# Query and key blocks transposed by VectorE and DMAs instead of TensorE, in a fused attention and feed-forward kernel

## The chip, the cores and the metric

The kernel runs on one core of one Trainium2 chip. The metric is the device time of one execution in microseconds. Three runs of the kernel before took 2517.53, 2520.3 and 2519.74 us; the median is 2519.74. One more execution was profiled; it took 2519.57 us, of which the profile covers a span of 2517.8.

## The reference

The input x has 4096 tokens (4 x 1024) of 512 features, all in fp32. Three residual stages follow one another:

```python
x = x + 0.5 * ffn(layernorm(x), W1, W2, W3)
x = x + attention(layernorm(x), wq, wk, wv, wo, inv_freq)
x = x + 0.5 * ffn(layernorm(x), W1, W2, W3)      # the same weights again

# ffn: hidden = silu(x @ W1.T) * (x @ W3.T)      # 2048 wide
#      return fwht(hidden) @ W2.T                # Walsh-Hadamard transform along the 2048
# attention: q, k, v of 16 heads of 32, rotary embedding on q and k;
#      scores = einsum('bshd,bstd->bsht', q, k) / sqrt(32)
#      return (softmax(scores) @ v) @ wo.T
```

The scores run over the heads of one token (s is kept, h meets t), so attention is a 16 x 16 product for each token, and no token meets another.

## The kernel before

**Tiling.** The tokens are cut into 8 tiles of 512, each of four blocks of 128 tokens; block g is block g % 4 of tile g // 4, 32 blocks in all. There are 16 passes (`PASSES`, 0 to 15), one for each tile and feed-forward stage, and the attention of the tiles is spread between them. Every matmul operand is kept as two fp32r parts, a high one (a copy that rounds) and a low one (the difference), and a product is three matmuls (`products`, L583 to L585: high x high, high x low, low x high).

**One pass.** `feed_forward(p)` has 16 steps, one for each 128 of the 2048 hidden features. In step n TensorE makes the up projections of the step, 24 matmuls of 128x512 into two banks of `gu`, then the down projection of the step before, 12 matmuls into the four banks of `acc`. ScalarE does SiLU from `gu` into `gated` (L1031), VectorE multiplies by the other bank (L1525, semaphore `s_h`), ScalarE copies the product as the high part of `hid` (L1039), VectorE subtracts for the low part (L1532, `s_hid_lo`), and TensorE uses both in the down projection. At the end of a pass the up projections of step 15 come first, then the down projections of steps 14 and 15 one after the other; only the last one (L583 to L585 into `acc`) waits at its start for the low part of step 15. SyncE loads each step's weights from device memory into two slots, about one step ahead.

**Attention on VectorE.** TensorE has only the projections. Scores and mixing of a block are 16 units on VectorE, each one product (L1258 or L1263) and one sum (L1270 or L1272) of 128x1024. `UNITS` says which units a pass has, and `units_by_step` deals them out over steps 0 to 14 so that VectorE's load is even, with costs for what stands beside them (`beside`): 2.5 for a unit, 0.55 for normalising a block at step 13. The exp of a block is on ScalarE, after the table load that it needs, and SiLU loads its own table again after it.

**The blocks of queries and keys.** For the pass p `new_subs(p)` lists two or three blocks whose queries, keys and values are projected in the gap before it. The first two are early (`early_subs`) when their first feed-forward stage is long done, 23 blocks in all. An early block is normalised by VectorE at step 13 of the pass ahead, into `prod[:, 2]` (`ln_apply`, L1174). TensorE transposes it in four squares of 128 (`transpose_sub`, L664) into PSUM, ScalarE copies that as the high part of `sub_xt` (`sub_high`, L915), VectorE subtracts for the low part (`sub_low`, L1138), and the projections of queries, keys and values use them. Where the transposes stand in TensorE's order depends on the gap: before a pass in `LATE` (3, 5, 7, 14) they are in `late_gap`, between the second and the third block of the output projection; else they are at the end of the pass ahead, between the up projections of step 15 and the down projection of step 14. One block is early before passes 2, 9 and 11, two before 3, 4, 5, 6, 7, 8, 10, 12, 13 and 14.

**The input of the feed-forward** goes another way already, where its pass isn't late (`MOVED`, nine passes): VectorE normalises it at steps 8 and 9, transposes it in squares of 32 (L1504), ScalarE issues four DMAs in each of steps 10 to 13 (`move`, L925), which put the squares in place within SBUF, ScalarE copies the high part at step 14 (`moved_high`, L932), and VectorE subtracts at step 15 (L1510).

Each engine runs its instructions in the order of the program. ScalarE issues DMAs from the same queue as its activations.

## Time and profile before

| | |
|---|---|
| median of three runs | 2519.74 us |
| the profiled execution, its span | 2519.57 us, 2517.8 us |
| TensorE matmuls busy | 2504.8 us (99%) |
| TensorE weight loads busy | 2074.0 us (82%) |
| VectorE busy | 2027.5 us (81%) |
| ScalarE busy | 528.8 us (21%) |
| GpSimd busy | 63.6 us (3%) |
| DMA queue of SyncE, of ScalarE: share of 16 engines | 45.8%, 3.4% |

A row of the profile names the line, the engine, the operation and what it writes and reads (out<-in). PE is TensorE, DVE VectorE, ACT ScalarE, POOL GpSimd, SP SyncE; ACTq and SPq are the DMA issues on those engines' queues. Matmuls overlap, so that a row's duration (0.39) is longer than the distance from one start to the next (0.227), and distances between starts are what counts. "[0.74 <-DVE prod L1174]" means that the engine sat idle for 0.74 us before the row, and that this instruction ended the idle time. A row without such a bracket followed the work before it at once.

### The profile page before, as it was taken

The numbers are of one execution on the slowest core, as the hardware profiler recorded it, in microseconds if no ns is written. First come the engines' busy times: TensorE is split into PE (matmuls) and PEld (weight loads), VectorE is DVE, ScalarE is ACT, GpSimd is POOL, SyncE is SP. The second block draws the span as 40 slices with busy tenths as digits, with TensorE's granted clock in tenths as the row PEclk, the third lists the DMA queues.
The fourth block names the chain that finished last, engine by engine and source line by source line (L and its number), as shares of the span: only waits on it lengthen the run. The fifth ranks groups of instructions, "written<-read, shape, count | busy, mean of one in ns | idle before, by whom it ended". The sixth has DMA issues, their size and how long they took to land.

```text
span 2517.8 us, 30105 instructions
## 1 busy us (share of the span) xinstructions
PE 2504.8 (99%) x11223; PEld 2074.0 (82%) x11223; DVE 2027.5 (81%) x2588; ACT 528.8 (21%) x810; POOL 63.6 (3%) x111
## 2 busy tenths in 40 slices
PE   9999999999999999999999999999999999999999
PEld 7878888888888888888888888888888888888887
DVE  9558978799786997979969889697886988978711
ACT  3322221222121221122212222122221212211211
POOL 0030000000000000000000000000000000000000
PEclk9999999999999999999999999999999999999999
DMA  9644635256452454525625546354562545535364
GB/s 340 251 188 177 213 138 190 101 199 202 169 207 76 176 210 162 203 100 200 203 89 208 167 180 211 118 213 146 200 208 76 186 165 210 185 115 200 134 219 165
DMA packets 112404, 446.89 MB, mean 177 GB/s; under 512 B 11201, under 2 KB 36033, under 8 KB 79041
## 3 DMA queue, kind: packets, MB, share of 16 engines
q1 hardware_dynamic: 82080, 420.26, 45.8%
q10 hardware_dynamic: 30240, 25.57, 3.4%
q8 instruction: 47, 0.77, 0.1%
q14 instruction: 37, 0.29, 0.0%
HBM read 402.79 MB, written 33.55 MB: 173 GB/s over the span
## 4 chain that ended last, share of the span: by engine, by line
PE 95%; DVE 4%; DMA 1%; ACT 0%; issue 0%; SPq 0%; DVEq 0%; ACTq 0%
PE gu L583 21%; PE gu L584 21%; PE gu L585 21%; PE acc L615 8%; PE acc L614 8%; PE acc L618 8%; PE acc L583 2%; PE acc L585 2%; PE acc L584 2%; PE acc L644 1%; DMA prod<-up_raw 1%; PE acc L709 1%; DVE prod L1263 1%; DVE mixed L1272 0%; DVE x L1202 0%; DVE w_up L1323 0%
## 5 line engine op out<-in xcount | busy, mean ns | idle before, releaser
L583 PE MATMUL gu<-xt,w_up 128*128 128x512 f32 x2048 | 798.6, 390 | 0.6 <-DVE xt L1138 0.4
L585 PE MATMUL gu<-xt,w_up 128*128 128x512 f32 x2048 | 796.9, 389 | 0.0
L584 PE MATMUL gu<-xt,w_up 128*128 128x512 f32 x2048 | 796.7, 389 | 0.0
L583 PEld LDWEIGHTS gu<-xt,w_up 128*128 128x128 f32 x2048 | 384.5, 188 | 81.6 <-issue 1.5
L584 PEld LDWEIGHTS gu<-xt,w_up 128*128 128x128 f32 x2048 | 384.5, 188 | 79.7
L585 PEld LDWEIGHTS gu<-xt,w_up 128*128 128x128 f32 x2048 | 384.5, 188 | 79.6
L1031 ACT ACTIVATE gated<-gu 128x512 f32<-128x512 f32 x240 | 143.6, 599 | 1137.8 <-PE gu L585 1137.8
L1525 DVE TENSOR_TENSOR gated<-gated,gu 128x512 f32<-128x512 f32 x240 | 163.2, 680 | 271.8 <-ACT gated L1031 271.2
L614 PE MATMUL acc<-w_down,hid 128*128 128x512 f32 x896 | 349.4, 390 | 0.0
L615 PE MATMUL acc<-w_down,hid 128*128 128x512 f32 x896 | 348.6, 389 | 0.0
L1258 DVE TENSOR_TENSOR prod<-tok 128x1024 f32<-128x1024 f32 x256 | 309.0, 1219 | 0.9
L1272 DVE TENSOR_REDUCE mixed<-prod 128x64 f32<-128x1024 f32 x256 | 309.6, 1211 | 0.0
L1270 DVE TENSOR_REDUCE scores<-prod 128x32 f32<-128x1024 f32 x256 | 309.2, 1211 | 0.0
L1263 DVE TENSOR_TENSOR prod<-scores,tok 128x1024 f32<-128x1024 f32 x256 | 307.4, 1212 | 1.5 <-DVE head_sum L1287 0.2
L618 PE MATMUL acc<-w_down,hid 128*128 128x512 f32 x896 | 239.5, 389 | 0.0
L1039 ACT ACTIVATE hid<-gated 128x512 fp32r<-128x512 f32 x240 | 151.8, 633 | 365.6 <-DVE gated L1525 365.2
L618 PEld LDWEIGHTS acc<-w_down,hid 128*128 128x128 f32 x896 | 168.2, 188 | 34.9
L614 PEld LDWEIGHTS acc<-w_down,hid 128*128 128x128 f32 x896 | 168.2, 188 | 34.7
L615 PEld LDWEIGHTS acc<-w_down,hid 128*128 128x128 f32 x896 | 168.3, 188 | 34.6
L1532 DVE TENSOR_TENSOR hid<-gated,hid 128x512 fp32r<-128x512 f32 x240 | 163.9, 683 | 20.3 <-ACT hid L1039 20.3
L583 PE MATMUL gu<-w_attn,sub_xt 128*128 128x512 f32 x232 | 91.2, 393 | 0.0
L585 PE MATMUL gu<-w_attn,sub_xt 128*128 128x512 f32 x232 | 90.3, 389 | 0.0
(141 smaller groups left out, 1956.0 us busy)
## 6 DMA issues: line engine op xcount, KB each, us to landing
w_up<-up_pairs SPq DMA_DIRECT2D x240, 1024.0 KB, 4.8
w_down<-down_pairs SPq DMA_DIRECT2D x240, 512.0 KB, 3.4
up_pairs<-w_up SPq DMA_DIRECT2D x16, 1024.0 KB, 4.9
xt<-tok ACTq DMA_DIRECT2D x144, 64.0 KB, 4.1
prod<-up_raw SPq DMA_DIRECT2D x16, 512.0 KB, 6.1
down_pairs<-w_attn SPq DMA_DIRECT2D x4, 2048.0 KB, 18.1
out<-x ACTq DMA_DIRECT2D x7, 1024.0 KB, 5.9
x<-x ACTq DMA_DIRECT2D x6, 1024.0 KB, 7.3
```

The costliest lines, as they stand in the source:

```text
L583: nc.tensor.matmul(o, w_hi, m_hi, start=first, stop=False)
L584: nc.tensor.matmul(o, w_hi, m_lo, start=False, stop=False)
L585: return nc.tensor.matmul(o, w_lo, m_hi, start=False, stop=last)
L614: nc.tensor.matmul(acc[:, s, :], h_hi[:, s * P:(s + 1) * P], hi, start=first, stop=False)
L615: nc.tensor.matmul(acc[:, s, :], h_hi[:, s * P:(s + 1) * P], lo, start=False, stop=False)
L618: ins = nc.tensor.matmul(acc[:, s, :], h_lo[:, s * P:(s + 1) * P], hi, start=False, stop=False)
L1258: return nc.vector.tensor_tensor(prod[:, buf, :].rearrange("p (h t d) -> p h t d", h=2, t=HEADS), wide(q[:, h:h + 2, None, :], 2, HEADS), ...
L1263: return nc.vector.tensor_tensor(prod[:, buf, :].rearrange("p (h d t) -> p h d t", h=2, d=HD), wide(scores[:, g % 2, h:h + 2, None, :], 2, ...
L1270: return nc.vector.tensor_reduce(scores[:, g % 2, h:h + 2, :], prod[:, buf, :].rearrange("p (h t d) -> p h t d", h=2, t=HEADS), AX.X, ALU.add)
L1272: return nc.vector.tensor_reduce(mixed[:, h:h + 2, :], prod[:, buf, :].rearrange("p (h d t) -> p h d t", h=2, d=HD), AX.X, ALU.add)
L1525: nc.vector.tensor_tensor(by_token(gated[:, u, :]), by_token(gated[:, u, :]), from_bank(gu[:, 2 * u + 1, :], p), ALU.mult).then_inc(s_h, 1)
L1532: nc.vector.tensor_tensor(low, gated[:, u, :], high.bitcast(FP32), ALU.subtract).then_inc(s_hid_lo, 1)
```

## The change

The 23 early blocks are no longer transposed by TensorE. They are normalised at step 11 of the pass ahead instead of step 13. VectorE then transposes each in place in squares of 32. At step 12 ScalarE issues a DMA for each block that writes it to device memory (`sub_squares`). At step 13 it waits for the writes and issues four DMAs for each block, which read the squares back in their places into the low part of `sub_xt`; the runs in device memory are 32 elements, 128 B. At step 14 ScalarE waits for the reads and copies the high part; VectorE subtracts at the place where it did before. The planner's cost for the normalisation goes from 0.55 at step 13 to 1.25 at step 11 for each block. The remaining 9 blocks keep their transposes on TensorE.

```diff
-X_STATS, X_APPLY, X_MOVE, X_SPLIT, Q_STATS, Q_APPLY = 6, 8, 10, 14, 10, 13
+X_STATS, X_APPLY, X_MOVE, X_SPLIT = 6, 8, 10, 14
+Q_STATS, Q_APPLY, Q_KEEP, Q_MOVE, Q_SPLIT = 10, 11, 12, 13, 14
...
+MOVED_SUBS = {g: at for at, g in enumerate(g for p in range(2, NP) for g in early_subs(p))}
...
-    beside[Q_APPLY] += 0.55 * len(early_subs(p + 1))
+    beside[Q_APPLY] += 1.25 * len(early_subs(p + 1))
...
+        sub_squares = nc.dram_tensor("sub_squares", [2, P, D], FP32).ap()
...
             def query_key(g, between=None):
-                split_ready("q", g, 0)
+                if g in MOVED_SUBS:
+                    pe.wait_ge(s_sub_lo, MOVED_SUBS[g] + 1)
+                else:
+                    split_ready("q", g, 0)
...
# late_gap on TensorE
-                output(p, 0)
-                output(p, 1)
-                if new:
-                    pe.wait_ge(s_added, SUBS * p)
-                    transpose_sub(new[0])
-                    transpose_sub(new[1])
-                output(p, 2)
-                output(p, 3)
+                for s in range(SUBS):
+                    output(p, s)
...
# feed_forward on TensorE, after the last up projection
-                    pe.wait_ge(s_h, n0 + HT - 1)
-                    for g in early_subs(after):
-                        transpose_sub(g)
                     down_step(last, 0, False, False)
...
# ScalarE
+            def keep_sub_squares(g):
+                act.wait_ge(s_sub_turned, MOVED_SUBS[g] + 1)
+                act.dma_start(sub_squares[new_subs(next_of(g)).index(g)], sub_normed(g)).then_inc(s_sub_kept, 16)
+
+            def move_sub(g):
+                later = max(early_subs(next_of(g)))
+                act.wait_ge(s_sub_kept, 16 * MOVED_SUBS[later] + 16)
+                squares = sub_squares[new_subs(next_of(g)).index(g)].rearrange("(q i) (k f j) -> f i k q j", q=QUADS, k=KT, f=QUADS)
+                for f in range(QUADS):
+                    act.dma_start(sub_split(g)[1][32 * f:32 * f + 32].bitcast(FP32).rearrange("p k (q j) -> p k q j", q=QUADS),
+                                  squares[f]).then_inc(s_sub_moved, 16)
+
+            def moved_sub_high(g):
+                later = max(early_subs(next_of(g)))
+                act.wait_ge(s_sub_moved, 16 * QUADS * (MOVED_SUBS[later] + 1))
+                high, low = sub_split(g)
+                nc.scalar.activation(high, low.bitcast(FP32), ACT.Copy).then_inc(s_sub_hi, 1)
...
# ScalarE, step n, behind the copy of the step's product
-                    if n == HT - 1 and after < NP and after not in LATE:
-                        for g in early_subs(after):
-                            sub_high(g)
...
                     if after in MOVED and X_MOVE <= n < X_MOVE + QUADS:
                         move(after, n - X_MOVE)
                     if after in MOVED and n == X_SPLIT:
                         moved_high(after)
+                    if after < NP and n == Q_KEEP:
+                        for g in early_subs(after):
+                            keep_sub_squares(g)
+                    if after < NP and n == Q_MOVE:
+                        for g in early_subs(after):
+                            move_sub(g)
+                    if after < NP and n == Q_SPLIT:
+                        for g in early_subs(after):
+                            moved_sub_high(g)
...
# VectorE
+            def moved_sub_low(g):
+                dve.wait_ge(s_sub_hi, MOVED_SUBS[g] + 1)
+                high, low = sub_split(g)
+                nc.vector.tensor_tensor(low, low.bitcast(FP32), high.bitcast(FP32), ALU.subtract).then_inc(s_sub_lo, 1)
...
                         if n == Q_APPLY:
+                            if after in MOVED:
+                                dve.wait_ge(s_turned, SUBS * MOVED[after] + SUBS)
                             for s, g in enumerate(early):
                                 ln_apply(key, s, sub_normed(g), x_of(g))
+                            for s, g in enumerate(early):
+                                dve.wait_ge(s_ln, ln_done(key, s))
+                                squares = sub_normed(g).rearrange("p (f j) -> p f j", j=32)
+                                nc.vector.transpose(squares, squares).then_inc(s_sub_turned, 1)
...
-                            sub_low(g)
+                            moved_sub_low(g)
```

## Rows read from the trace of the kernel before

**Rows 1.** The page: busy time of TensorE, and the chain that ended last
```profile
PE 2504.8 (99%) x11223; PEld 2074.0 (82%) x11223; DVE 2027.5 (81%) x2588; ACT 528.8 (21%) x810; POOL 63.6 (3%) x111
...
PE 95%; DVE 4%; DMA 1%; ACT 0%; issue 0%; SPq 0%; DVEq 0%; ACTq 0%
```

**Rows 2.** Timeline of TensorE, end of pass 3: start, duration, engine, line, operation
```profile
626.28 1.03 PE L664 MATMUL gu<-ident,prod 128*128 128x128 f32 x8
627.07 0.48 PE L614 MATMUL acc<-w_down,hid 128*128 128x512 f32 x1
627.39 0.40 PE L615 MATMUL acc<-w_down,hid 128*128 128x512 f32 x1
```

**Rows 3.** Timeline of VectorE and TensorE, steps 14 and 15 of pass 3
```profile
619.47 0.68 DVE L1525 TENSOR_TENSOR gated<-gated,gu 128x512 f32<-128x512 f32 x1
...
627.11 0.69 DVE L1525 TENSOR_TENSOR gated<-gated,gu 128x512 f32<-128x512 f32 x1 [0.71 <-ACT gated L1031]
628.50 0.69 DVE L1532 TENSOR_TENSOR hid<-gated,hid 128x512 fp32r<-128x512 f32 x1 [0.70 <-ACT hid L1039]
...
629.89 0.39 PE L583 MATMUL acc<-w_down,hid 128*128 128x512 f32 x1
```

**Rows 4.** Timeline of ScalarE and its queue, pass 3, steps 12 and 13
```profile
608.26 2.55 ACTq L925 DMA_DIRECT2D xt<-tok  x4
610.90 1.28 ACT L1031 ACT_TABLE_LOAD   x1 [2.23 <-issue]
612.19 0.60 ACT L1031 ACTIVATE gated<-gu 128x512 f32<-128x512 f32 x1
```

**Rows 5.** Timeline of TensorE, gap before pass 3
```profile
476.62 1.03 PE L664 MATMUL acc<-ident,prod 128*128 128x128 f32 x8
```

**Rows 6.** Timelines of VectorE and TensorE, end of pass 9
```profile
1577.04 0.69 DVE L1532 TENSOR_TENSOR hid<-gated,hid 128x512 fp32r<-128x512 f32 x1 [0.70 <-ACT hid L1039]
...
1577.88 0.47 PE L583 MATMUL acc<-w_down,hid 128*128 128x512 f32 x1 [0.80 <-DVE hid L1532]
```

**Rows 7.** Timelines of VectorE and TensorE, end of pass 1
```profile
317.33 0.69 DVE L1532 TENSOR_TENSOR hid<-gated,hid 128x512 fp32r<-128x512 f32 x1 [0.70 <-ACT hid L1039]
...
318.33 0.40 PE L583 MATMUL acc<-w_down,hid 128*128 128x512 f32 x1
...
324.71 0.66 PE L664 MATMUL gu<-ident,prod 128*128 128x128 f32 x4 [0.74 <-DVE prod L1174]
```

**Rows 8.** Groups by line: busy us, mean ns, then idle time before them
```profile
L1504 DVE STREAM_TRANSPOSE tok<-prod 128x512 f32<-128x512 f32 x36 | 23.3, 686 | 0.0
L1138 DVE TENSOR_TENSOR sub_xt<-gu,sub_xt 128x512 fp32r<-128x512 f32 x18 | 11.8, 684 | 4.1 <-ACT sub_xt L915 4.1
```

**Rows 9.** DMA issues by line (ns min/median/max), and one in SyncE's timeline
```profile
L925 ACTq DMA_DIRECT2D xt<-tok x144: 592/622/1267, 275.9 to 2041.0; - x144
...
L987 ACTq DMA_DIRECT2D tok<-w2t x1: 437/437/437, 30.4 to 30.4; - x1
...
111.25 1.02 SPq L531 DMA_DIRECT2D down_pairs<-w_attn  x1
```

**Rows 10.** Timelines of ScalarE and VectorE, steps 13 to 15 of passes 5, 7, 9
```profile
931.50 0.63 ACT L1039 ACTIVATE hid<-gated 128x512 fp32r<-128x512 f32 x1 [1.98 <-DVE gated L1525]
945.88 0.69 DVE L1525 TENSOR_TENSOR gated<-gated,gu 128x512 f32<-128x512 f32 x1 [0.79 <-ACT gated L1031]
...
1243.14 0.63 ACT L1039 ACTIVATE hid<-gated 128x512 fp32r<-128x512 f32 x1 [3.54 <-DVE gated L1525]
1249.06 0.68 DVE L1525 TENSOR_TENSOR gated<-gated,gu 128x512 f32<-128x512 f32 x1
...
1565.97 0.69 DVE L1525 TENSOR_TENSOR gated<-gated,gu 128x512 f32<-128x512 f32 x1 [1.15 <-ACT gated L1031]
```

**Rows 11.** DMA view, 450 to 620 us: ScalarE's queue; landing times of L925
```profile
q10 hardware_dynamic: 2304, 1.05, 2.7%
...
DMA to landing us min/median/max: 2.0/4.1/6.3
```

More of the change, by code:

```diff
@@ L156, in transposed @@
         elif p in LATE:
-            order += att + [("q", g, 0) for g in new[:2]] + [("x", p, k) for k in range(KT)]
+            order += att + [("x", p, k) for k in range(KT)]
         else:
-            order += [("q", g, 0) for g in early_subs(p)]
             order += [("q", g, 0) for j, g in enumerate(new[:2]) if not is_early(p, j)] + att
@@ L342, in build @@
         s_moved_lo = sem("s_moved_lo")
+        s_sub_turned = sem("s_sub_turned")
+        s_sub_kept = sem("s_sub_kept")
+        s_sub_moved = sem("s_sub_moved")
+        s_sub_hi = sem("s_sub_hi")
+        s_sub_lo = sem("s_sub_lo")
         s_wo = sem("s_wo")
@@ L762, in late_gap @@
                     query_key(new[0])
-                    split_ready("q", new[1], 0)
                 pe.wait_ge(s_ln, LN_FROM["x", p] + SUBS)
@@ L926, in move, with next_of @@
                                   squares[32 * q:32 * q + 32, :, f, :]).then_inc(s_moved, 16)
+            def next_of(g):
+                return next(p for p in range(2, NP) if g in new_subs(p))
+            def keep_sub_squares(g):
[13 more added lines that the diff above has]
+                nc.scalar.activation(high, low.bitcast(FP32), ACT.Copy).then_inc(s_sub_hi, 1)
             def moved_high(p):
@@ L1066, in gap @@
                     attention_high(p)
-                    for g in new[:2]:
-                        sub_high(g)
                     for k in range(KT):
@@ L1556, in late_gap @@
                         for g in new[:2]:
-                            sub_low(g)
+                            moved_sub_low(g)
                 ln_means(key, at, last_of(key))
@@ L1609, in early_gap @@
                         dve.wait_ge(s_added, SUBS * (p - 1) + 1)
-                    else:
-                        dve.wait_ge(s_tp, TP["q", new[0], 0] + 1)
                     sub_stats(just[0])
```

## The prediction

> **What bounds the kernel now.** I read the page's first and fourth parts first: TensorE is busy 2504.8 of 2517.8 us and 95% of the chain that ended last is its own work, VectorE's share is 4% [rows 1]. So time can only be won by taking work from TensorE, and only where no other engine is waiting just behind. The second view is therefore the timeline at the ends of the passes (pass p is the p-th run of the 16-step feed-forward loop, 0 to 15), where the removed transposes stand. Within a pass a step takes 8.16 us (36 matmuls at 0.227), ScalarE's SiLU of a step starts as soon as TensorE has finished that step's up projections, and VectorE multiplies 0.63 us later [rows 3]. What the reader is to see there: the last down projection of a pass waits for the split of the last hidden step, a chain of SiLU, multiply, copy, subtract that starts when TensorE ends the last up projection and takes 2.7 us. The transposes lie inside that time, beside the chain.
>
> **What is removed.** 23 blocks of four transposes. Eight of them hold TensorE from 626.28 to 627.07 and make the next matmul 0.09 longer (a pitch of 0.31 for 0.23), so 0.88 for two blocks, 0.44 for one [rows 2]. 23 blocks are 10.1 us (23 x 0.44), the most there is. How much of it counts depends on the place:
>
> - Before the four late passes (3, 5, 7, 14) the eight transposes stand between two output projections [rows 5]. The chain behind them (add, statistics, normalisation, transposes of x) starts from the end of the output projections and moves along with them; VectorE's subtractions for the blocks no longer wait for a transpose. 4 x 0.88 = 3.5 us won.
> - At the ends of passes 3, 5, 11 and 12 (two blocks) the last down projection starts 0.70 after VectorE's split of the last hidden step ends (629.89 against 629.19); the other three show 0.71. Where TensorE really waits, it starts 0.15 after that end (1577.88 after 1577.73) and its first matmul is 0.07 longer [rows 3, 6]. So only 0.70 - 0.15 - 0.07 = 0.48 of the 0.88 can be won in each.
> - Passes 7, 9 and 10: the start already follows at 0.15 [rows 6]. Nothing won.
> - Passes 1 and 8 (one block): 0.31 after the split. Later in that gap TensorE waits for VectorE's normalisation of the second block (0.74 idle), and that hangs on the same split [rows 7]. Nothing won.
>
> With everything else free: 3.5 + 4 x 0.48 = 5.4 us, not 10.1.
>
> **What is added on VectorE.** 23 transposes of 128x512 (0.69 each, 0.60 in a row) [rows 8]. The subtraction stays what it was; from a source in SBUF it costs the same (0.69 at 628.50 in rows 3, 0.684 from PSUM). So 1.2 us for a pass with two blocks. The planner's cost at step 11 also shifts attention units (2.3 us each) by a step or two: pass 3 had 3, 2, 3 units in steps 12 to 14 and gets 2, 3, 3, and the unit that goes to step 13 is the first on values of block 6, with its row sums and a product more (4.1 us). VectorE came to step 14 late before (multiply at 619.47, no idle time ahead of it) and had 0.71 idle before the last multiply [rows 3]. Now it gets there at about 621.7: the last multiply and the split after it come 1.4 later even if no DMA costs anything. In passes 5, 9, 11 and 12 idle time of 0.8 to 2.8 in steps 13 to 15 takes the shift.
>
> **What is added on ScalarE.** Its two copies for a block (0.6 each) move a step ahead, into 3.8 us of idle time. What counts are its DMA issues. An issue holds ScalarE's queue: in pass 3 four of them from 608.26 to 610.81 kept the table load for SiLU waiting until 610.90, and SiLU came at 612.19, two microseconds behind TensorE [rows 4]. Step 12 gets one or two issues more; step 13 gets four to eight more behind the four that are there, with two blocks twelve in all. The price of one is the first unknown. The trace has 0.62 to 0.64 for the moves of x (32 partitions, in pieces), 0.44 for a load from device memory in 2048 pieces, and 1.02 for a store in 512 pieces pushed behind others [rows 9]. I take 0.637, the pitch of the move, which the new one is nearest to in engine and form. Then SiLU of step 14 can't start before the copy of step 13 + 12 x 0.637 + 0.09, the multiply 0.63 later: copy + 8.36 us (5.81 with one block). From a multiply in step 14 with three units to the last one VectorE needs 6.9 (619.47 to 627.11 less 0.71). Pass by pass, the room at 3, 5, 11, 12 being 0.70 - 0.15 = 0.55:
>
> - 3: the copy at 612.5, behind the exp that now stands in step 13, issues to 620.1, a table load of 1.3, the multiply at 622.1, the last at 629.0 for 627.11. Late by 1.9, less the room, and 0.07: +1.4.
> - 7: 1243.14 + 8.36 = 1251.5 for 1249.06, and no idle time follows: +2.4.
> - 9: the copy at 1558.5 (0.5 earlier, a unit less before it), 1566.9 for 1565.97, the rest full: +0.9.
> - 10, one block: 1722.82 + 5.81 = 1728.6 for 1728.28: +0.35.
> - 5: 931.5 + 8.36 = 939.9, the last multiply at 946.8 for 945.88, 0.9 less the room: +0.4 (5, 7 and 9 in [rows 10], whose form 10 and 12 repeat).
> - 12: the same by 0.4 less: 0. 11 has two units in step 14 and 2.8 idle: -0.5. 1 and 8: 0.
>
> Sum at the pass ends: 1.4 + 2.4 + 0.9 + 0.35 + 0.4 - 0.5 = +5.0. Before the late passes (ends of 2, 4, 6, 13) there are eight issues without the moves of x, 5.1 us, and 1.3 us of room before the down projection: nothing.
>
> **The landing.** ScalarE waits in step 14 for the reads, 4096 pieces of 128 B for two blocks, 256 to each DMA engine. Pieces of 512 B on this queue take 32 ns (2304 packets, 2.7% of 16 engines over 170 us) [rows 11]. A quarter of that by bytes gives 2 us, the whole of it 8.2. In pass 3 the first push is at 616.1; the shortest landing is 2.0 [rows 11]. The copies must be over by 626.5, so the reads in by 625.3: 2 us of transfer never shows, 8.2 us ends at 626.3, one microsecond late in some four passes, +3. I take the lower half: hidden behind the pushes. The weights on the other queue have room: the last down slab is pushed at about 310 and lands in 3.4, used at 318.
>
> Here the Trainium skill speaks against the change: its page DMA: Bandwidth & Descriptors, section Specifications, names 512 B as the least size for line rate, with a read-modify-write below it. No row of this trace has pieces of 128 B to confirm it. By that rule the 256 pieces would cost more than 32 ns each, which is rival 3.
>
> **Sum.** +5.0 - 3.5 = +1.5 us on the profiled execution's 2519.57 us (span 2517.8 and 1.8 around it), which is 0.17 below the median of 2519.74: 2521.1.
>
> **The rivals.**
> 1. *Cheap pushes*: at 0.43 an issue, as the load in 2048 pieces, twelve take 6.0 us. Pass 3 still loses 1.0 to VectorE and pass 7 0.8 to the queue; 11 wins 0.5, 5 and 12 about 0.3 each, 9 and 10 nothing: +0.7 - 3.5 = -2.8, 2516.8. With issues and VectorE's shift hidden entirely, -5.4: 2514.2. For it: so many pieces were pushed at that price. Against: the four-dimensional pattern and the 32 partitions.
> 2. *The push grows with the pieces, and the kernel is slower*: place, step 13 on ScalarE's queue in the ends with moves of x; price, each of the new issues at 1.0, as the stores pushed behind others. Twelve take 2.9 us more in two-block passes, 1.5 in one-block ones: 3 loses 4.3, 5 3.3, 7 5.3, 9 3.8, 10 1.8, 11 0.4, 12 2.9, and 6 and 13 now 1.9 each beyond their room: +25.6 - 3.5 = +22, 2542. It decides from 0.72 an issue on, where the sum passes 5 us (4.4 us for each 0.1); at 0.8 it is +8.7. For it: four times the pieces, twelve pushes in a row. Against: 2048 pieces were pushed in 0.44.
> 3. *Small pieces read slowly*: at twice the row of 512 B, 64 ns for 128 B, 256 pieces take 16.4 us from the first push; ScalarE's copies end 9.2 us behind SiLU 15 in six passes and 3.3 beyond the room in four: +65, 2585.
>
> **How the numbers follow.** Own forecast 0.52, rival 1 0.20, rival 2 0.24, rival 3 0.04. About 0.2% (5 us) is what can be told from no change. Rival 1 passes -5 only at its far end: faster 0.08. Slower are rivals 2 and 3 and the upper part of my own (an issue of 0.72, late landings): 0.38. Within: 0.54. The range runs from 2515 (rival 1 near its end) to 2532 (0.88 an issue); beyond it lie half of rival 2 and rival 3.
>
> **What would show it.** Right: no transposes between the last up and down projections, a wait of TensorE for the split of hidden step 15 at most two-block ends, the issues of the new reads at 0.6 each in step 13, SiLU 14 behind its up projection in passes 3, 7 and 9, late gaps 0.88 shorter. Wrong: an issue near 0.4 or 1.0 (terms of step 13), SiLU 15 late with ScalarE waiting for a DMA (the landing), or gaps after pass ends that shrink by the full 0.88.

## The result: 9 microseconds slower, and the profile after

The changed kernel takes 2529.27 us (median of 7, 2528.13 to 2532.96), the kernel before 2519.70 beside it on the same chip (7 runs, 2517.53 to 2520.6). The ratio is 1.0043, interval 1.0034 to 1.0052: slower by 0.43%. The forecast was 2521.1 with a range of 2515 to 2532, so the time lies in the range, 8 us above the forecast. Of the three outcomes it had given 0.54 to no clear change, 0.38 to slower and 0.08 to faster; slower came. The profiled execution took 2528.13 us with a span of 2526.3, 8.5 more than before.

The page of the changed kernel, to be held against [rows 1] (busy time, and the chain that ended last):

```profile
PE 2500.8 (99%) x11131; PEld 2068.3 (82%) x11131; DVE 2040.9 (81%) x2611; ACT 529.1 (21%) x810; POOL 63.6 (3%) x111
...
PE 81%; DVE 14%; ACTq 2%; ACT 1%; issue 1%; DMA 1%; SPq 0%; DVEq 0%
```

The change's own DMA issues by line, writes and reads (nanoseconds of one as least, median, most; first and last start), to be held against [rows 9]:

```profile
L934 ACTq DMA_DIRECT2D sub_squares<-prod x23: 326/574/974, 295.4 to 2186.6; - x23
...
L942 ACTq DMA_DIRECT2D sub_xt<-sub_squares x92: 564/657/1902, 303.5 to 2202.8; - x92
```

TensorE's busy time fell by 4.0 us (2504.8 to 2500.8), with 92 matmuls fewer, and yet the program is longer. VectorE's share of the chain went from 4% to 14% and ScalarE's queue (ACTq), which had 0%, is on it with 2%: TensorE now waits for a chain that goes back over VectorE to a ScalarE that was pushing DMAs. It is the queue's 2% that matters: in experiments 2 and 4 below, which are faster than the kernel before, VectorE has 16% and 13% of the chain and the queue 1% and 0%. The view of waits names the place (engine, operation, released by; us in all, times, longest). Its first two lines are idle time of ScalarE ahead of SiLU and of SiLU's table load, ended by nothing but ScalarE's own pushes:

```profile
ACT gated L1054 <- issue: 44.4, 6, 7.9
...
ACT L1054 <- issue: 26.6, 7, 6.8
...
PE acc L591 <- DVE hid L1570: 14.3, 11, 3.7
```

The last line is TensorE's wait for the split of hidden step 15; it was 1.0 us in 2 cases before. Each case is one end of a pass; three of the eleven are of 0.17 (passes 1, 8 and 15). TensorE's timeline has them as idle time (in brackets) ahead of the last down projection; the other eight are the ends of passes 3, 5, 7, 9, 10, 11, 12 and 13:

```profile
629.51 0.47 PE L591 MATMUL acc<-w_down,hid 128*128 128x512 f32 x1 [1.69 <-DVE hid L1570]
948.03 0.47 PE L591 MATMUL acc<-w_down,hid 128*128 128x512 f32 x1 [1.15 <-DVE hid L1570]
1260.32 0.47 PE L591 MATMUL acc<-w_down,hid 128*128 128x512 f32 x1 [3.74 <-DVE hid L1570]
1582.59 0.77 PE L591 MATMUL acc<-w_down,hid 128*128 128x512 f32 x1 [3.35 <-DVE hid L1570]
1745.97 0.74 PE L591 MATMUL acc<-w_down,hid 128*128 128x512 f32 x1 [2.19 <-DVE hid L1570]
1895.40 0.47 PE L591 MATMUL acc<-w_down,hid 128*128 128x512 f32 x1 [0.17 <-DVE hid L1570]
2064.91 0.47 PE L591 MATMUL acc<-w_down,hid 128*128 128x512 f32 x1 [1.06 <-DVE hid L1570]
2214.60 0.47 PE L591 MATMUL acc<-w_down,hid 128*128 128x512 f32 x1 [0.39 <-DVE hid L1570]
```

Where the longest wait comes from is seen in ScalarE's timeline, here steps 13 and 14 of pass 7:

```profile
1241.72 0.63 ACT L1062 ACTIVATE hid<-gated 128x512 fp32r<-128x512 f32 x1 [3.54 <-DVE gated L1563]
1241.72 2.60 ACTq L926 DMA_DIRECT2D xt<-tok  x4
1244.36 5.42 ACTq L942 DMA_DIRECT2D sub_xt<-sub_squares  x8
1249.89 0.60 ACT L1054 ACTIVATE gated<-gu 128x512 f32<-128x512 f32 x1 [7.54 <-issue]
```

The reader is to see that ScalarE computes nothing for 7.54 us because twelve DMAs are ahead of SiLU in program order. In the kernel before it idled 3.39 us here, for its input; now the input was ready 4.15 us before SiLU 14 began. SiLU 14 comes 8.17 after the copy of step 13 (the forecast had 8.36 to the multiply 0.63 later, so 7.73). Not every wait is the queue's: with the reads on another queue (experiment 4) TensorE still waits 1.64 at the end of pass 3 and 1.69 at that of pass 9, for VectorE.

**What nobody had on the list.** The first matmul behind the waits of 3.35 and 2.19 takes 0.77 and 0.74 instead of 0.47. The view of windows shows why (columns: window, us, busy time of PE, PEld, DVE, ACT, POOL, then the granted clock, DMA share, GB/s); first the end of pass 7, then those of 9 and 10:

```profile
1260.00:1262.00 2.00, 1.68 (x6) 1.43 (x7) 2.00 (x4) 0.00 (x0) 0.00 (x0) 0.83 0.03 8
1262.00:1264.00 2.00, 2.00 (x6) 1.52 (x6) 2.00 (x3) 0.00 (x0) 0.00 (x0) 0.50 0.00 0
1264.00:1266.00 2.00, 2.00 (x9) 1.61 (x8) 1.97 (x5) 0.00 (x0) 0.75 (x2) 0.82 0.00 0
...
1582.00:1584.00 2.00, 1.41 (x3) 1.16 (x4) 2.00 (x4) 0.00 (x0) 0.00 (x0) 0.54 0.18 72
1584.00:1586.00 2.00, 2.00 (x7) 1.62 (x6) 2.00 (x3) 0.00 (x0) 0.00 (x0) 0.61 0.00 0
1746.00:1748.00 2.00, 2.00 (x5) 1.61 (x6) 2.00 (x3) 0.00 (x0) 0.00 (x0) 0.50 0.35 143
1748.00:1750.00 2.00, 2.00 (x7) 1.56 (x7) 1.97 (x3) 0.00 (x0) 0.00 (x0) 0.65 0.00 0
```

The granted clock goes to 0.50, which is 1.2 GHz for 2.4, right behind three waits of 3.74, 3.35 and 2.19 us, and TensorE then does 6 matmuls in 2 us where it did 11 at about the same place before:

```profile
1260.00:1262.00 2.00, 2.00 (x11) 1.62 (x10) 2.00 (x2) 0.00 (x0) 0.00 (x0) 1.00 0.79 266
```

(this row is of the kernel before, in which the clock was at 1.00 from 178 us to the end). The kernel before had one such place, ahead of pass 1, and it was there to be read; its timeline and window:

```profile
172.89 0.77 PE L583 MATMUL gu<-w_attn,xt 128*128 128x512 f32 x1 [2.54 <-DVE tok L1241]
```

```profile
174.00:176.00 2.00, 2.00 (x6) 1.53 (x5) 2.00 (x5) 0.00 (x0) 0.00 (x0) 0.50 0.00 0
```

So these three waits are paid twice: once as they pass, once as low clock behind them.

**Where the 9 us are.** The start of the last down projection, counted from SiLU 0 of its pass, gives what a pass end lost by waiting; the shift of SiLU 0 from one pass to the next gives all of it. What the second has over the first is the clock, where the clock fell. Differences after minus before, in us, all from the profiled execution of each kernel:

| end of pass | forecast | start of last down | shift to the next pass | rest |
|---|---|---|---|---|
| 3 | +1.4 | +0.96 | +1.09 | 0.1 |
| 5 | +0.4 | +0.41 | +0.53 | 0.1 |
| 7 | +2.4 | +2.89 | +4.49 | 1.6 (low clock) |
| 9 | +0.9 | +1.66 | +3.05 | 1.4 (low clock) |
| 10 | +0.35 | +1.79 | +2.38 | 0.6 (low clock) |
| 11 | -0.5 | -0.57 | -0.46 | 0.1 |
| 12 | 0 | +0.33 | +0.43 | 0.1 |
| 13 | 0 | +1.04 | +0.11, with the late gap's -0.93 in it | 0 |
| 2, 4, 6 with late gaps | -0.88 each | 0 | -0.92, -0.79, -0.91 | 0 |

The shifts sum to +9.0 over passes 1 to 15 (SiLU 0 of pass 1 comes 0.45 earlier than before, that of pass 15 8.56 later): ends with waits +9, late gaps -3.55 (the three and pass 13's 0.93), low clock +3.6, which is part of the +9. The low clock lasts about as long at all three places; in pass 10 it costs only 0.6, because a wait of 0.85 of the kernel before, for VectorE's normalisation later in that gap, is gone.

### The profile page after: what moved, and what is told of

The parts are those of the page before. It is cut to its first block, busy times and chain, and to the rows that moved or that the text cites. A ratio compares the mean times of both kernels' runs of the same rounds, so it can differ in the third digit from the quotient of the medians.

```text
span 2526.3 us, 30055 instructions
## 1 busy us (share of the span) xinstructions
PE 2500.8 (99%) x11131; PEld 2068.3 (82%) x11131; DVE 2040.9 (81%) x2611; ACT 529.1 (21%) x810; POOL 63.6 (3%) x111
## 3 DMA queue, kind: packets, MB, share of 16 engines
q10 hardware_dynamic: 82128, 37.64, 5.5%
## 4 chain that ended last, share of the span: by engine, by line
PE 81%; DVE 14%; ACTq 2%; ACT 1%; issue 1%; DMA 1%; SPq 0%; DVEq 0%
PE gu L591 18%; PE gu L592 18%; PE gu L593 18%; PE acc L623 7%; PE acc L626 7%; PE acc L622 7%; DVE mixed L1304 2%; DVE prod L1295 2%; PE acc L591 2%; PE acc L592 2%; PE acc L593 2%; DVE scores L1302 2%; DVE prod L1290 2%; ACTq L942 1%; DVE hid L1570 1%; DVE gated L1563 1%
```

## The experiments

Each kernel was timed in five rounds against the kernel before on the same chip; times are medians. Four kernels change who pushes DMAs, when, how many or for which blocks; three take one suspected cost by itself; one puts the findings together. The changed kernel was timed in other rounds than these, where the kernel before stood at 2519.70 for 2519.37 (experiments 1 to 4) and 2519.40 (5 to 8) here, so a difference to the changed kernel is good to some tenths.

**1. Only the blocks before the late passes.** The eight blocks ahead of passes 3, 5, 7 and 14 keep the new path, the other 15 go back to TensorE.

```diff
-MOVED_SUBS = {g: at for at, g in enumerate(g for p in range(2, NP) for g in early_subs(p))}
+MOVED_SUBS = {g: at for at, g in enumerate(g for p in range(2, NP) if p in LATE for g in early_subs(p))}
...
-    beside[Q_APPLY] += 1.25 * len(early_subs(p + 1))
+    if p + 1 in LATE:
+        beside[Q_APPLY] += 1.25 * len(early_subs(p + 1))
+    else:
+        beside[13] += 0.55 * len(early_subs(p + 1))
```

> Only the 8 blocks ahead of passes 3, 5, 7 and 14 go over VectorE and device memory; the other 15 are transposed by TensorE as in the kernel before, with their normalization at step 13 and its cost in the planner at 0.55. ScalarE's queue (my theory): passes 1, 4, 6, 8 to 13 are left as before, so the waits of 3.35, 2.19, 1.06 and 0.39 at the ends of passes 9, 10, 12 and 13 go, and so does the low clock behind the first two. The late gaps keep their -0.8 to -0.9 each (-3.6 in all); pass 2 ends as in the changed kernel (0), pass 4 and 6 too, pass 13 with eight reads at most +1.0. Sum -3.6 to -2.6: 2516 to 2517. VectorE's own work (rival): the same here, since the late passes' ends showed nothing of it. Small reads that crowd the DMA (rival): no different from my theory for these passes, since pass 2, 4, 6 and 13 have them all; a gain of less than 2 would speak for it.

Measured: 2515.67 us, ratio 0.9984 (0.9975 to 0.9993). Faster than the kernel before. The shifts to SiLU 0 of passes 3, 5, 7 and 14 are -0.92, -0.97, -0.91 and -0.89, 3.7 in all, and every other pass end stands within 0.02 of before. The term "4 x 0.88" of the prediction was right, and the loss of the changed kernel sits in the other 15 blocks, but for pass 13. There the reads are pushed here too, in the same order behind the exp, in 5.46 us for 7.05, and nothing is lost:

```profile
2185.09 5.46 ACTq L949 DMA_DIRECT2D sub_xt<-sub_squares  x8
```

**2. The issues spread.** All 23 blocks, each part a step earlier, the second block's reads a step behind the first's.

```diff
-Q_STATS, Q_APPLY, Q_KEEP, Q_MOVE, Q_SPLIT = 10, 11, 12, 13, 14
+Q_STATS, Q_APPLY, Q_KEEP, Q_MOVE, Q_SPLIT = 9, 10, 11, 12, 14
...
-                    if after < NP and n == Q_MOVE:
-                        for g in early_subs(after):
-                            move_sub(g)
+                    if after < NP and Q_MOVE <= n < Q_MOVE + len(early_subs(after)):
+                        move_sub(early_subs(after)[n - Q_MOVE])
```

> The whole change, but each part one step earlier (statistics 9, normalization and squares 10, write 11), and the reads of the first block at step 12, of the second at step 13, so that ScalarE issues at most 8 DMAs in a step beside x's moves rather than 12 (4 of x's and 4 of the blocks'). ScalarE's queue: step 13 has 8 issues rather than 12 (5.1 rather than 7.6), step 12 has 8 rather than 4 or 6; the lateness of SiLU 14 (1.7 to 4.2 in passes 3, 5, 7, 9, 10, 12) falls by about 2.5, so the waits of TensorE at the last down projection of passes 3, 7, 9, 10 fall from 11.0 in all to about 2, the low clock behind them (3 times 3.4) goes with them, and the time falls by 8 to 11: 2518 to 2521. If step 12's load now holds SiLU 13, half of that. VectorE's own work: it stays the same or is worse by the earlier normalization: 2529 or more. Small reads and their landing: no fewer of them, 2529.

Measured: 2515.91 us, ratio 0.9988 (0.9979 to 0.9997): 13.4 below the changed kernel, more than expected. The same DMAs with the same pieces cost little once at most eight stand in one step. ScalarE in step 13 of pass 7 now:

```profile
1241.30 2.56 ACTq L926 DMA_DIRECT2D xt<-tok  x4
1243.89 2.67 ACTq L942 DMA_DIRECT2D sub_xt<-sub_squares  x4
1246.66 0.60 ACT L1054 ACTIVATE gated<-gu 128x512 f32<-128x512 f32 x1 [4.74 <-issue]
```

SiLU 14 is 1.34 late against its up projection, not 4.15, the wait of TensorE is 0.94, and the low clock is gone at all three places. VectorE's extra work is unchanged here (2040.8 us busy), so it did not make the kernel slow.

**3. Five DMAs for ten.** Four writes put the squares in place for both blocks, one contiguous read brings them.

```diff
-                act.dma_start(sub_squares[new_subs(next_of(g)).index(g)], sub_normed(g)).then_inc(s_sub_kept, 16)
+                for q in range(QUADS):
+                    act.dma_start(places[q], squares[32 * q:32 * q + 32]).then_inc(s_sub_kept, 16)
...
-                for f in range(QUADS):
-                    act.dma_start(sub_split(g)[1][32 * f:32 * f + 32].bitcast(FP32).rearrange("p k (q j) -> p k q j", q=QUADS),
-                                  squares[f]).then_inc(s_sub_moved, 16)
+                act.dma_start(sub_xt[:, 0:count, 1].bitcast(FP32).rearrange("p g k n -> p g (k n)"),
+                              squares_of(p).rearrange("p (g n) -> p g n", g=count)).then_inc(s_sub_moved, 16)
```

> The squares are put in their places by the write: four writes at step 12 for both blocks (pieces of 128 bytes on the side of device memory), and one read at step 13 with runs of 2 KB: 5 DMAs in a two-block pass rather than 10, and in step 13 one issue beside x's four rather than eight. ScalarE's queue: step 13 issues 5 (3.2) rather than 12 (7.6), step 12 issues 8 (5.1) rather than 6 (3.6): SiLU 14 is on time, the waits at the last down projection go nearly all (12 of 14.3) and the three stretches of low clock (3.6) with them; what is left is VectorE's part, some 1 to 3. Time 2517 to 2521. Small pieces (rival): there are as many as before, now in writes, which should be worse for device memory if anything: 2529 or more.

Measured: 2520.39 us, ratio 1.0006 (0.9997 to 1.0015). The number fell into what was expected, but not in the expected way: fewer DMAs weren't cheaper ones. ScalarE's timeline in pass 9:

```profile
1551.49 3.35 ACTq L943 DMA_DIRECT2D sub_squares<-prod  x4
...
1564.60 0.58 ACTq L948 DMA_DIRECT2D sub_xt<-sub_squares  x1
1565.29 0.60 ACT L1059 ACTIVATE gated<-gu 128x512 f32<-128x512 f32 x1 [8.36 <-DMA sub_squares<-prod]
```

A write of 1024 pieces holds the queue for 0.81 to 1.44 on the average of its four (3.35 for the four here, 5.78 in pass 6). And in pass 9 ScalarE computed nothing for 8.36 us. The moves of x were pushed until 1559.55; for the 5.05 us from there to the read it waited for the writes to land, and the read was pushed 9.8 us after the last of them. That one end has the longest wait of TensorE of all runs (4.26) and costs 5.08, of which 2.79 are the later start and 2.3 the low clock (0.50 in three windows of 2 us from 1576). Without it this kernel would stand at about 2515 (an estimate), where experiments 1, 2 and 4 are: the shifts of its other passes, from pass 1 on, sum to -4.5.

**4. SyncE pushes the reads.** Nothing else is changed; SyncE's loops are unrolled for it.

```diff
                 up_weights(HT - 1, 1)
+                if b + 1 < NP:
+                    for g in early_subs(b + 1):
+                        move_sub(g)
                 down_weights(HT - 2, 0)
...
-                    if after < NP and n == Q_MOVE:
-                        for g in early_subs(after):
-                            move_sub(g)
```

> The same write by ScalarE at step 12 and the same reads with the same pieces, but the reads are issued by SyncE, behind its last load of up weights of the pass (up projection 14 done, about the time of step 13 to 14), so that ScalarE issues only x's moves in step 13. SyncE's loops over steps and passes are unrolled for it. ScalarE's queue: SiLU 14 is on time in passes 3, 5, 7, 9, 10, 12, the waits of 14.3 fall to 3 or less and the low clock goes: 2517 to 2521. If the reads land too late for the high parts at step 14 (issue of 8 at 0.6 = 5 plus 3 landing), SiLU 15 and the copy behind it are late instead by 1 to 4 in two-block passes, and the gain is half. VectorE's own work, or small reads that crowd the DMA: 2529, unchanged.

Measured: 2515.22 us, ratio 0.9983 (0.9974 to 0.9992): 14.1 below the changed kernel, again more than expected. Pass 7, queues and the last down projection:

```profile
1237.95 6.44 SPq L594 DMA_DIRECT2D sub_xt<-sub_squares  x8
...
1241.44 2.55 ACTq L940 DMA_DIRECT2D xt<-tok  x4
...
1245.45 0.60 ACT L1068 ACTIVATE gated<-gu 128x512 f32<-128x512 f32 x1 [3.39 <-PE gu L607]
...
1256.47 0.47 PE L605 MATMUL acc<-w_down,hid 128*128 128x512 f32 x1 [0.17 <-DVE hid L1581]
```

SiLU 14 waits for TensorE again, not for a push, at every pass end to within 0.01. The eight reads take no less time to push (6.44 for 5.42) and no less to land (4.1 at the median, 2.9 in the changed kernel); SyncE has the time. This is the run that settles it: the same data, the same pieces, the same writes, the same work on VectorE, and 14 us less, by the queue. The unrolled loops of SyncE are its one other difference, and experiment 2 wins 13.4 without them.

**5. The waits filled.** In the changed kernel, matmuls into a bank whose content nobody reads any more stand in the waits of passes 7, 9 and 10.

```diff
                     down_step(last, 0, False, False)
+                    if after in (8, 10, 11):
+                        pe.wait_ge(s_h, n0 + HT - 1)
+                        for _ in range({8: 12, 10: 10, 11: 6}[after]):
+                            nc.tensor.matmul(gu[:, 0, :], w_attn[:, 0, 0, 0, 0:P], w_attn[:, 0, 0, 0, :], start=True, stop=True)
```

> The changed kernel, with matmuls whose result nobody reads put between the last two down projections ahead of passes 8, 10 and 11 (12, 10 and 6 of them, 0.23 each, so 2.8, 2.3 and 1.4), inside waits of 3.74, 3.35 and 2.19: TensorE then idles for about 1 in each instead. Nothing that it waits for comes earlier. If the wait itself calls forth the low clock (my reading), the three stretches of 3.4 at the lower level go and the time falls by about 3.6, to 2525.7. If the low clock comes from something else at these places (DMA traffic, VectorE and ScalarE both busy), it stays: 2529.3, and if the fill makes the down projection late, it is more.

Measured: 2525.49 us, ratio 1.0022 (1.0013 to 1.0032): 3.8 below the changed kernel (3.5 with the two kernels before set equal) by work that nobody needs. TensorE's timeline at the end of pass 7:

```profile
1259.99 2.88 PE L887 MATMUL gu<-w_attn 128*128 128x512 f32 x12
1263.89 0.47 PE L591 MATMUL acc<-w_down,hid 128*128 128x512 f32 x1 [1.02 <-DVE hid L1574]
```

And the windows there:

```profile
1262.00:1264.00 2.00, 0.98 (x5) 0.52 (x4) 1.30 (x3) 0.63 (x1) 0.00 (x0) 1.00 0.50 199
1264.00:1266.00 2.00, 2.00 (x9) 1.66 (x10) 2.00 (x4) 0.00 (x0) 0.00 (x0) 1.00 0.04 8
```

The last down projection starts as late as in the changed kernel (+2.89), but the shift to pass 8 is +2.87 rather than +4.49; at passes 9 and 10 the two agree likewise (2.01 and 1.99, 0.80 and 0.54). In this execution the push in pass 3 took 6.78 rather than 5.64, TensorE idled 2.81 there where nothing was filled, and the clock fell at that place instead:

```profile
632.00:634.00 2.00, 2.00 (x6) 1.54 (x6) 2.00 (x4) 0.00 (x0) 0.00 (x0) 0.50 0.04 8
```

That end cost 3.79, 1.7 more than its later start. So the low clock follows the wait, wherever the wait is. In this pair of executions the fill is worth 3.9 (the shift less the later start, at passes 7, 9 and 10); pass 3 loses 2.7 more than in the changed kernel's execution and pass 9 starts its last down projection 0.35 later, passes 10 and 13 start it 1.0 earlier each, by pushes of other lengths. That the medians differ by nearly the 3.6 of the low clock is in part luck.

**6. Whole rows.** The same number of reads with the same bytes, in runs of 2 KB. The kernel leaves out that the squares are put in their places, so that the 23 blocks' queries and keys are not the reference's.

```diff
-                squares = sub_squares[new_subs(next_of(g)).index(g)].rearrange("(q i) (k f j) -> f i k q j", q=QUADS, k=KT, f=QUADS)
+                squares = sub_squares[new_subs(next_of(g)).index(g)].rearrange("(f i) n -> f i n", f=QUADS)
...
-                    act.dma_start(sub_split(g)[1][32 * f:32 * f + 32].bitcast(FP32).rearrange("p k (q j) -> p k q j", q=QUADS),
+                    act.dma_start(sub_split(g)[1][32 * f:32 * f + 32].bitcast(FP32).rearrange("p k n -> p (k n)"),
```

> The changed kernel with the same number of reads of the same 64 KB each, but each read takes whole rows of 2 KB rather than sixteen pieces of 128 bytes a row, so the squares of the 23 blocks are not put in their places. The issue costs what a DMA costs (my theory): eight issues stay at 5 or more (0.6 each), SiLU 14 is as late as before: 2528 to 2530. The push grows with the pieces (a rival of the prediction): the issues fall to about 0.35 each, as the writes' do, and the time to 2521. Small pieces crowd the DMA: the landings fall from 2.9 to 2.3 and nothing else changes.

Measured: 2520.31 us, ratio 1.0003 (0.9994 to 1.0012). My theory of a fixed price fell here; the rival's number, 2521, was right. The reads of this kernel, to be held against L942 above, and their landing:

```profile
L942 ACTq DMA_DIRECT2D sub_xt<-sub_squares x92: 312/443/1872, 304.6 to 2195.4; - x92
...
DMA to landing us min/median/max: 1.9/2.9/5.1
```

A median push of 0.443 for 0.657, eight in pass 7 in 3.91 for 5.42. The landing has the same median, 2.9, in both. So the form of a read is paid on the queue that pushes it, not on the way. Whether it is the number of pieces (32 for 512) or the shape of the pattern that is paid, this run doesn't take apart: both changed. Against the number alone speak 2048 pieces pushed in 0.437 and the moves of x, fewer pieces and 0.622 [rows 9].

**7. VectorE's share alone.** The kernel before, with the earlier normalization, the transposes in squares and the planner's new costs. It leaves out the writes and reads that would put the squares in place, so that TensorE transposes blocks that are not the reference's.

```diff
-X_STATS, X_APPLY, X_MOVE, X_SPLIT, Q_STATS, Q_APPLY = 6, 8, 10, 14, 10, 13
+X_STATS, X_APPLY, X_MOVE, X_SPLIT, Q_STATS, Q_APPLY = 6, 8, 10, 14, 10, 11
...
-    beside[Q_APPLY] += 0.55 * len(early_subs(p + 1))
+    beside[Q_APPLY] += 1.25 * len(early_subs(p + 1))
...
+                            for s, g in enumerate(early):
+                                dve.wait_ge(s_ln, ln_done(key, s))
+                                squares = sub_normed(g).rearrange("p (f j) -> p f j", j=32)
+                                chain.mark(nc.vector.transpose(squares, squares))
```

> The kernel before with only VectorE's share of the change: normalization at step 11, its squares transposed in place (so the 23 blocks' data is out of place), 1.25 in the planner; the write, the reads and the splits from them are left out, and TensorE transposes the 23 blocks as before. My theory: VectorE has room everywhere but at the end of pass 3, where the last multiply comes 1.4 late beside TensorE's transposes that still follow it: +1.0 to +1.9, and less than 0.5 elsewhere: 2520.5 to 2521.5. If VectorE's own work made the changed kernel slow, most of its 9.8 is here: 2526 or more.

Measured: 2520.44 us, ratio 1.0005 (0.9996 to 1.0014), 1.0 above the kernel before in these rounds (2519.40). The trace has it in one place: from pass 1 on, the shift of the end of pass 3 is +1.04, every other is within 0.25. The rival of VectorE's own work is out; the claim that pass 3 loses "even if no DMA costs anything" stands.

**8. Both findings together.** Experiment 4, and the two blocks ahead of pass 4 left to TensorE.

```diff
+ANEW = {p for p in range(2, NP) if p != 4}
-MOVED_SUBS = {g: at for at, g in enumerate(g for p in range(2, NP) for g in early_subs(p))}
+MOVED_SUBS = {g: at for at, g in enumerate(g for p in range(2, NP) if p in ANEW for g in early_subs(p))}
```

> The reads issued by SyncE as in the experiment before it, and the two blocks ahead of pass 4 transposed by TensorE as in the kernel before. That experiment lost time at one place alone, +1.0 at the end of pass 3, where TensorE waited 1.64 for VectorE. If that is the price of VectorE's shifted units there, it goes: 2514.2 (1.0 below 2515.2). If it comes from the reads on SyncE's queue, it stays only where reads remain, and pass 3 gains too; the two are told apart by the multiply of step 15 in pass 3, which was 1.5 late and should be on time at 16.9 behind SiLU 13 or earlier.

Measured: 2514.34 us, ratio 0.9979 (0.9970 to 0.9988), the lowest of all: 0.2% faster than the kernel before. The last multiply of pass 3 is on time, as in [rows 3], with TensorE's transposes beside it:

```profile
626.25 1.03 PE L691 MATMUL gu<-ident,prod 128*128 128x128 f32 x8
...
627.08 0.69 DVE L1585 TENSOR_TENSOR gated<-gated,gu 128x512 f32<-128x512 f32 x1 [0.70 <-ACT gated L1077]
```

Its shift to pass 4 is 0.00 for +1.00 in experiment 4. That this is 0.9 below experiment 4 is within what two medians can differ by; the trace, not the ratio, says that it is gained. That the 1.0 was the price of VectorE's shifted work and not of the reads is shown by experiment 7, which has no reads and loses the same there.

## Why the prediction was right in kind and short in size, step by step

- *What bounds the kernel*, TensorE with a chain beside its last up projection: right. All that was lost was lost at that chain's end.
- *What is removed.* The late gaps, 3.5: right (3.55 in the changed kernel, 3.7 in experiment 1). The ends of passes 5, 11 and 12 at 0.48 each: right for the start of the last down projection once nothing hides them (0.47, 0.56, 0.47 in experiment 4), of which 0.35, 0.44 and 0.39 reach the next pass. Passes 7 and 10, forecast at nothing, give 0.67 and 0.22 in experiment 4: VectorE's units move too, and in pass 7 its last multiply is 16.95 behind SiLU 13 for 17.63. The most that the idea had to give, -5.4 in the forecast, is -5.1 measured (experiment 8, with 21 of the 23 blocks; -5.7 in its trace). That the totals agree is luck in part: pass 3's 0.48 never came, passes 7 and 10 stand in its place.
- *What is added on VectorE*: +1.2 us per two-block pass and a loss in pass 3. Right; experiment 7 gives +1.0 in all and the changed kernel +0.96 there. The forecast of 1.4 for that end was worked out from the queue's push, and in the profiled execution the push had no part in it: VectorE's last multiply is 18.48 behind SiLU 13 in the changed kernel and 18.44 in experiments 4 and 7, where ScalarE pushes no reads.
- *The landing*: right. ScalarE waited for a read once, 2.2 us in pass 7, where VectorE's last multiply had no idle time in front of it and so did not wait for ScalarE. The prediction's first push, at 616.1, doesn't follow from its own copy at 612.5 and four moves (615.05), and nothing in the sum used it; the trace has 612.78. By the profile's page, ScalarE's queue went from 30240 packets and 3.4% of 16 engines to 82128 and 5.5%, so 51888 packets more took 2.1% of 16 x 2526 us, 849 us, about 16 ns each, the writes included. Rival 3, at 64 ns, is out. The Trainium skill's page DMA: Bandwidth & Descriptors, section Specifications, names 512 B as the least size for line rate. The trace agrees per byte: 128 B in 16 ns is half the rate of 512 B in 32 ns [rows 11]. What did not come is the prediction's step from there to more than 32 ns for each piece.
- *What is added on ScalarE*: the term that was mis-sized. The forecast took 0.637 for an issue, "the pitch of the move". Eight reads in a row take 5.4 to 5.95 in eight of ten cases but 6.81 in pass 4 and 7.05 in pass 13, and the four of pass 10 take 3.92; over the 92 of them it is 68 us, 0.74 each. The mean hides two things. Asked for one by one, 76 of the 92 pushes last 0.56 to 0.67, 0.68 from one start to the next (5.42 for eight in pass 7); twelve last over 0.75, the longest 1.81 (pass 13) and 1.90, the third of the four in pass 10:

```profile
1732.16 0.66 ACTq L942 DMA_DIRECT2D sub_xt<-sub_squares  x1
1732.85 1.90 ACTq L942 DMA_DIRECT2D sub_xt<-sub_squares  x1
1734.78 0.66 ACTq L942 DMA_DIRECT2D sub_xt<-sub_squares  x1
```

  Where the long ones fall differs from one execution to the next: in experiment 5, which pushes the same reads, the longest (1.85) is in pass 3, and passes 10 and 13 take 2.67 and 5.80. The later starts of the last down projection sum to +8.5 where the forecast had +5.0. The 3.5 between them are 1.4 in pass 10, 1.0 in pass 13, 0.8 in pass 9, 0.5 in pass 7, 0.3 in pass 12 and -0.4 in pass 3. The prediction's own slope (4.4 us for each 0.1) would make 4.6 of the 0.10 above 0.637, but that slope doesn't hold pass 13, without which the later starts are 2.5 above the forecast. Without the low clock the changed kernel would stand at about 2525.0 (+9.0 less 3.6 on top of 2519.6, an estimate), and experiment 5 measured 2525.5. Rival 2 had named 0.72 as the point from which it decides, and the mean push passed it. Its price of 1.0 was too high, the forecast's too low; its mechanism, a push that grows with the pieces, is shown only as far as experiment 6 goes: whole rows are pushed faster.
- *Before the late passes, nothing*: wrong in pass 13 of the profiled execution, +1.04. There an exp stands behind the copy of step 13, its table load and 0.42 of work come before the reads in the queue, and SiLU 14 needs another table load behind them:

```profile
2195.06 1.28 ACT L978 ACT_TABLE_LOAD   x1
2196.45 0.42 ACT L978 ACTIVATE scores<-scores 128x256 f32<-128x256 f32 x1
2196.46 7.05 ACTq L942 DMA_DIRECT2D sub_xt<-sub_squares  x8
2203.60 1.28 ACT L1054 ACT_TABLE_LOAD   x1 [6.72 <-issue]
2204.89 0.60 ACT L1054 ACTIVATE gated<-gu 128x512 f32<-128x512 f32 x1
```

  The exp was worked out for pass 3 and not looked for in 13. It takes the room but doesn't cost by itself: with the same order and pushes of 5.46 and 5.80 experiments 1 and 5 lose nothing there (SiLU 14 is 2.1 and 2.4 late for 3.7). The 1.04 is the long push's.
- *Missing altogether*: the clock, +3.6. The forecast priced a wait at its length, although the row at 172.89 of the kernel before shows a wait of 2.54 with the low clock behind it. Shown by the windows and by experiment 5.

In sum: forecast +1.5 on the span; measured +8.5. Of the difference of 7 the later starts make 3.5, nearly all by the price of the pushes, and the low clock 3.6. That the time lies in the range all the same is luck in part: the upper end of 2532 was worked out from an issue of 0.88, and what brought the time near it was an issue of 0.74 and a clock that the range did not hold.

The cause of the push's price is not settled beyond experiment 6. With whole rows one alone takes 0.32 and eight in a row 0.49 each; why the second differs from the first, and why single pushes take 1.8 to 1.9 (one in pass 10 with whole rows too, 1.87), no run takes apart.

## What to carry to other kernels

A DMA is paid twice, on the way and on the engine that pushes it. Before a change adds issues, count all that stand between two compute instructions of that engine, times what a push of that shape takes in a row, with room for a long one, and hold the sum against the time to the next instruction that others wait for; here moving eight of twelve to a queue with nothing urgent turned +0.4% into -0.2%. A wait of the matmul engine can cost more than its length: look in the trace for waits as long as the one forecast, and read the granted clock behind them. And a saving is worth only the room to the next chain: of 10.1 us of removed transposes (9.2 in experiment 8), 5.1 came out at best, and 3.7 of it from the eight of 23 blocks that stood where nothing else ran.

## What the runs showed of the hardware that was not expected

- **Low clock behind short waits.** TensorE's idle time at a pass end and the granted clock in the windows behind it, in all the runs here: 4.26, 3.74, 3.35, 2.81, 2.23, 2.19 and 1.91 were followed by 0.50 (experiment 3, changed kernel twice, experiment 5, experiment 6, changed kernel, experiment 6), and so was the 2.5 ahead of pass 1 in every run; 1.74, 1.72, 1.69 (four times), 1.64 (three times) and all shorter ones were followed by 1.00. In the changed kernel the three stretches cost 1.6, 1.4 and 0.6. The Trainium skill's page TensorE: Matmul & The Clock Gate, section What's actually happening, says that the clock has two levels and that recent activity sets which. The traces agree: the windows show 0.50 and 1.00, and values between them only where a change falls into the window.
- **The push pays for the form of the DMA.** A read of 64 KB takes its queue 0.66 in 512 pieces of 128 B and 0.44 in 32 of 2 KB, at the median; a write of 128 KB in 1024 pieces 0.81 to 1.44 on the average of four; but a load in 2048 pieces took 0.437 [rows 9], so the number of pieces alone doesn't give the price. On SyncE's queue the same reads take 0.637 at the median, near the 0.657 on ScalarE's. Single pushes of the same form reach 1.8 to 1.9 on both.
- **Issue time is not small beside the transfer.** The Trainium skill's page DMA: Bandwidth & Descriptors, section Issuing engines are not separate DMA queues, says that spreading DMAs over engines saves only the time to initiate them, "which is usually small relative to the DMA itself". The first half agrees: landings did not change for the better in experiment 4 (4.1 for 2.9). The second doesn't fit here: one push is 0.74 on the average, a quarter of the 2.9 in which a read lands, eight in a row hold the queue for 5.4 to 7.05, and taking them off ScalarE is the 14 us of experiment 4.
- **A scattered write can land late.** In experiment 3, 9.8 us from the last push of four at 1554.8 to the first read at 1564.6, where 4.8 is the median from push to landing of that kernel's writes and reads.
